# Macaron block (feed-forward, attention, feed-forward): transposes three and values four steps behind the scores, copies swapped between ScalarE and VectorE, side jobs spread anew

## The reference

```python
x = x + 0.5 * ffn(layernorm(x))          # x: 4 x 1024 tokens x 128
x = x + attn(layernorm(x))
x = x + 0.5 * ffn(layernorm(x))

def attn(x):                             # HEADS = 16, HEAD_DIM = 64, WINDOW = 64
    h = silu(x @ W1.T + b1) @ W2.T + b2
    q, k, v = split(h @ Wg.T + bg, 3)    # 3 * 16 * 64 columns
    dots = einsum('bhid,bhjd->bhij', q, k) * HEAD_DIM ** (-0.5)
    dots = where(j >= i + WINDOW, -inf, dots)
    out = einsum('bhij,bhjd->bhid', softmax(dots), v)
    return out @ Wo.T + bo

def ffn(x):                              # hidden 384
    return (silu(x @ wg.T) * (x @ wu.T)) @ wd.T
```

## Time and profile before

| | |
|---|---|
| median of 3 runs | 1632.81 us (1631.2 to 1634.49) |
| profiled execution | 1628.43 us, its span 1626.6 us, mean granted clock 0.976 |
| TensorE | 1439.0 us busy (88%), weight loads 1113.7 (68%) |
| GpSimd | 990.7 us (61%) |
| VectorE | 970.6 us (60%) |
| ScalarE | 776.3 us (48%) |
| DMA | 18 GB/s mean |

### The profile page before, as it was taken

The page is one execution under the profiler, slowest core; times in us unless marked ns, Lnnn a source line. Parts: engine busy times, 40 slices in busy tenths (PEclk is TensorE's granted clock), DMA queues, the critical chain, the costliest instruction groups (busy, mean ns, idle before and its releaser), DMA issues.

```text
span 1626.6 us, 38540 instructions
## 1 busy us (share of the span) xinstructions
PE 1439.0 (88%) x13330; PEld 1113.7 (68%) x13330; DVE 970.6 (60%) x1886; ACT 776.3 (48%) x1827; POOL 990.7 (61%) x592
## 2 busy tenths in 40 slices
PE   4767999999999999999999999999999999998676
PEld 3543777777777777777777777777777777777566
DVE  5653666666666666566666656666666656665444
ACT  2323555555555455554555555555555455454332
POOL 2231767677666667666676766677666666667410
PEclk9995999999999999999999999999999999999978
DMA  3100000000000000000000000000000000000000
GB/s 96 36 0 18 19 19 19 18 18 18 18 18 18 13 5 18 18 18 18 18 18 18 18 18 18 18 18 18 18 18 18 18 1 17 18 0 1 1 26 26
DMA packets 30571, 29.42 MB, mean 18 GB/s; under 512 B 6993, under 2 KB 25298, under 8 KB 30546
## 3 DMA queue, kind: packets, MB, share of 16 engines
q1 hardware_dynamic: 30546, 29.09, 5.9%
HBM read 8.07 MB, written 2.10 MB: 6 GB/s over the span
## 4 chain that ended last, share of the span: by engine, by line
PE 55%; issue 17%; DVE 13%; POOL 7%; ACT 6%; DVEq 1%; DMA 1%; ACTq 0%; POOLq 0%; SPq 0%
PE banks L773 16%; PE banks L754 15%; PE banks L789 8%; PE banks L719 6%; POOL probs L324 6%; ACT probs L389 5%; DVE probst L549 4%; DVE negmax L537 4%; PE banks L655 4%; PE banks L742 2%; PE banks L723 2%; DVE hidden L492 1%; PE banks L734 1%; POOL rstd_ln L295 1%; DVE xn_ln L478 1%
## 5 line engine op out<-in xcount | busy, mean ns | idle before, releaser
L324 POOL TENSOR_SCALAR probs<-probs,recips 128x704 f32<-128x704 f32 (+7 forms) x512 | 947.6, 1864 | 452.5 <-DVE recips L542 452.5
L537 DVE TENSOR_REDUCE negmax<-banks 128x1 f32<-128x704 f32 (+7 forms) x512 | 392.6, 808 | 129.8 <-PE banks L754 129.8
L773 PE MATMUL banks<-ident,probs 128*128 128x128 f32 x2752 | 391.4, 281 | 43.2 <-DVE probst L549 22.6
L397 ACT ACTIVATE probst<-banks 128x512 f32<-128x512 f32 (+1 forms) x320 | 177.4, 555 | 516.2 <-PE banks L773 516.2
L389 ACT ACTIVATE probs<-banks,negmax 128x704 f32<-128x704 f32 (+7 forms) x512 | 397.2, 785 | 44.5 <-DVE negmax L537 44.5
L773 PEld LDWEIGHTS banks<-ident,probs 128*128 128x128 f32 x2752 | 293.2, 141 | 130.3 <-issue 69.3
L549 DVE COPY probst<-banks 128x512 f32<-128x512 f32 (+1 forms) x416 | 276.6, 665 | 171.8 <-PE banks L773 169.8
L789 PE MATMUL banks<-probst,vs 128*64 128x128 f32 x5504 | 357.0, 277 | 0.8 <-ACT probst L397 0.8
L789 PEld LDWEIGHTS banks<-probst,vs 128*64 128x64 f32 x5504 | 295.3, 137 | 37.6 <-issue 22.5
L754 PE MATMUL banks<-kt,qt 64*128 64x512 f32 (+4 forms) x2496 | 298.3, 365 | 3.1 <-issue 3.1
L754 PEld LDWEIGHTS banks<-kt,qt 64*128 64x128 f32 x2496 | 206.0, 186 | 50.5 <-issue 5.8
(11 more groups left out here) (58 smaller groups left out, 881.1 us busy)
## 6 DMA issues: line engine op xcount, KB each, us to landing
hslot<-h_sb SPq DMA_DIRECT2D x32, 512.0 KB, 3.2
wslot<-in_wqkvt SPq DMA_DIRECT2D x32, 128.0 KB, 3.0
wslot<-wq_sb SPq DMA_DIRECT2D x32, 64.0 KB, 2.6
y<-xres SPq DMA_DIRECT2D x8, 256.0 KB, 2.3
wo_sb<-in_wot SPq DMA_DIRECT2D x1, 512.0 KB
wq_sb<-in_wqkvt SPq DMA_DIRECT2D x1, 512.0 KB
bslot<-bqk_sb SPq DMA_DIRECT2D x32, 1.0 KB, 1.9
iload<-in_wgatet SPq DMA_DIRECT2D x1, 192.0 KB, 2.4
```

The lines of the kernel that those rows point to most:

```text
L324: nc.gpsimd.tensor_scalar(here, here, recips[:, c, h:h + 1], None, ALU.mult).then_inc(normed.sem, 1)
L397: nc.scalar.activation(probst[c % 2][:, 4 * g:4 * g + w, :].rearrange("p t q -> p (t q)"), banks[:, TRANSPOSED[g % 2], 0:w * P], ACT.Copy) ...
L537: nc.vector.tensor_reduce(negmax[:, c, h:h + 1], src, AX.X, ALU.max, negate=True).then_inc(maxed.sem, 1)
L773: last = nc.tensor.transpose(banks[:, TRANSPOSED[g % 2], (t - 4 * g) * P:(t - 4 * g + 1) * P], probs[c, h][:, kb * P:(kb + 1) * P], ident[:])
```

## The change

`T_LAG` goes from 2 to 3 and `PV_LAG` from 3 to 4. ScalarE copies the even groups of transposes and VectorE the odd ones. On ScalarE the copy of group 0 stands ahead of the exponentials. On VectorE the reciprocal now stands ahead of the step's jobs, and the first job ahead of the copy of group 3. On TensorE the first job of a step comes after the value products, a second one after all transposes. The jobs get new steps; v0 and v1 are made in the turn that uses them, and no longer before the first turn; o1 joins o2 and o3 behind the drain.

```diff
-    T_LAG, PV_LAG = 2, 3
+    T_LAG, PV_LAG = 3, 4
-    JOBS = {0: ["k0"], 1: ["o2", "q0"], 2: ["k1"], 3: ["o3", "q1"], 4: ["v0"], 5: ["o0"], 6: ["v1"], 7: ["o1"]}
+    JOBS = {0: ["o1"], 1: ["v0"], 2: ["o2"], 3: ["v1"], 4: ["o3", "k0"], 5: ["q0"], 6: ["o0", "k1"], 7: ["q1"]}
...
-        taken = [T("taken_vector", [(c, g) for c in range(STEPS) for g in range(0, groups[c], 2)]),
-                 T("taken_scalar", [(c, g) for c in range(STEPS) for g in range(1, groups[c], 2)])]
+        taken = [T("taken_scalar", [(c, g) for c in range(STEPS) for g in range(0, groups[c], 2)]),
+                 T("taken_vector", [(c, g) for c in range(STEPS) for g in range(1, groups[c], 2)])]
...
-        def job_turn(job, c, i):
-
-            return i + 1 if job[0] in "kqv" else i - 1 if job in ("o2", "o3") else i
+        def job_turn(job, i):
+
+            return i + 1 if job[0] in "kq" else i - 1 if job in ("o1", "o2", "o3") else i
+
+        def runs(job, carry, more):
+            return more if job[0] in "kq" else carry or job[0] == "v" or job == "o0"
...
@@ ScalarE, step @@
-                if turning and groups[tc] > 1:
-                    take(tc, 1, ti)
-                if here:
-                    exps(c, i)
+                if turning:
+                    take(tc, 0, ti)
+                exps(c, i)
                 if carry or c >= PV_LAG:
                     attention_out(ac, ai)
-                if turning and groups[tc] > 3:
-                    take(tc, 3, ti)
+                if turning and groups[tc] > 2:
+                    take(tc, 2, ti)
...
@@ VectorE, step @@
                 row_max(c, i)
-                if turning:
-                    take(tc, 0, ti)
-                for job in JOBS[c]:
-                    if job[0] == "o" and (carry or job in ("o0", "o1")):
-                        add_output(job, job_turn(job, c, i))
-                if turning and groups[tc] > 2:
-                    take(tc, 2, ti)
+                if turning and groups[tc] > 1:
+                    take(tc, 1, ti)
                 invert(c, i)
-                for job in JOBS[c]:
-                    if job[0] == "v" and more:
-                        values(job, i + 1, 1 - r)
-                    if job[0] in "kq" and more:
-                        queries_keys_low(job, i + 1, 1 - r)
+                for job in JOBS[c][:1]:
+                    evict(job, i, r, carry, more)
+                if turning and groups[tc] > 3:
+                    take(tc, 3, ti)
+                for job in JOBS[c][1:]:
+                    evict(job, i, r, carry, more)
...
-            values("v0", 0, 0)
-            values("v1", 0, 0)
...
-            add_output("o2", TURNS - 1)
-            add_output("o3", TURNS - 1)
+            for name in ("o1", "o2", "o3"):
+                add_output(name, TURNS - 1)
...
@@ TensorE @@
-                if c == 0:
-                    pe.wait_ge(v_done.sem, v_done.after("v1", i))
+
+                pe.wait_ge(v_done.sem, v_done.after("v0" if blocks[c] <= 4 else "v1", i))
...
                 score(c, i, r)
                 if turning:
                     turns_of(tc, ti, (0, 1))
-                for job in JOBS[c]:
-                    if job[0] == "o":
-                        do(job)
                 if attending:
                     attend(ac, ai, r if c >= PV_LAG else 1 - r)
+                do(JOBS[c][0])
                 if turning:
                     turns_of(tc, ti, (2, 3))
-                for job in JOBS[c]:
-                    if job[0] != "o":
-                        do(job)
+                for job in JOBS[c][1:]:
+                    do(job)
...
-            for name in proj.events:
+            for name in ("k0", "q0", "k1", "q1"):
```

More of the change, by code:

```diff
@@ L435, in _ @@
             for c in range(PV_LAG):
-                tail_step = c
                 ti, tc = back(TURNS, c, T_LAG)
@@ L439, in _ @@
                 if c < T_LAG:
-                    take(tc, 1, ti)
+                    take(tc, 0, ti)
                 attention_out(ac, ai)
-                if c < T_LAG:
-                    take(tc, 3, ti)
+                if c < T_LAG and groups[tc] > 2:
+                    take(tc, 2, ti)
             copy_transposed(pd, "ln1", 0)
@@ L580, in step, with evict @@
                 row_max(c, i)
[L581 to L593 removed]
+                if turning and groups[tc] > 1:
+                    take(tc, 1, ti)
+                invert(c, i)
+                for job in JOBS[c][:1]:
[4 more added lines that the diff above has]
+                    evict(job, i, r, carry, more)
+            def evict(job, i, r, carry, more):
+                if not runs(job, carry, more):
+                    return
+                if job[0] == "o":
+                    add_output(job, job_turn(job, i))
+                elif job[0] == "v":
+                    values(job, i, r)
+                else:
+                    queries_keys_low(job, i + 1, 1 - r)
             for name in qk_done.events:
                 queries_keys_low(name, 0, 0)
[L597 to L598 removed]
             for c in range(STEPS):
@@ L802, in step @@
                 turning, attending = carry or c >= T_LAG, carry or c >= PV_LAG
-                def runs(job):
-                    return more if job[0] in "kqv" else carry or job in ("o0", "o1")
                 def do(job):
-                    if not runs(job):
+                    if not runs(job, carry, more):
                         return
                     k = JOB_ORDER.index((c, job))
-                    earlier = [(s, name, i) for s, name in JOB_ORDER[:k] if runs(name)]
-                    s, name, t = earlier[-1] if earlier else (*JOB_ORDER[-1], i - 1)
-                    misc_read(name, job_turn(name, s, t))
-                    n = job_turn(job, c, i)
-                    if job[0] in "kqv":
-                        project(job, n, 1 - r)
+                    earlier = [(name, i) for _, name in JOB_ORDER[:k] if runs(name, carry, more)]
+                    name, t = earlier[-1] if earlier else (JOB_ORDER[-1][1], i - 1)
+                    misc_read(name, job_turn(name, t))
+                    n = job_turn(job, i)
+                    if job[0] == "o":
+                        output(job, n)
                     else:
-                        output(job, n)
+                        project(job, n, r if job[0] == "v" else 1 - r)
                 score(c, i, r)
@@ L864, in _ @@
                     turns_of(tc, ti, (2, 3))
+            misc_read("o0", TURNS - 1)
+            output("o1", TURNS - 1)
             misc_read("o1", TURNS - 1)
```

24 lines of the change are left out of this document (12 added, 12 removed).

## The result

| | before | after |
|---|---|---|
| median | 1632.38 us, 4 runs | 1779.7 us, 4 runs (1774.93 to 1783.96) |
| ratio | | 1.09, 95% interval 1.0868 to 1.0932 |
| span of the profiled execution, granted clock | 1626.6 us, 0.976 | 1779.7 us, 0.938 |
| one turn in the middle (28 turns) | 43.02 us | 48.15 us |

The change costs 147.3 us. I had forecast 40, and a range that ended at 1702. The page after the change: the busy times, the granted clock in 40 slices, and the queue that brings instructions (packets, MB, share).

A forecast was written before the change was run, and what follows sets the result against it. TensorE's one stream of matmuls was taken as the bound. Turns of 44.4 us, 1.4 more, add 42 us over 30 turns; one-time terms -2. With 40 added to the 1632.8 median, the forecast was 1673 us, range 1650 to 1702.

The forecast's parts named there:

- the holes: TensorE's idle gaps in each middle turn: forecast to grow from 4.4 us to 5.63 us, making a turn 44.4 us.
- the terms that come once: Prologue without v0 and v1 saves 5.7 us, turn 0 costs 0.8 and the drain 2.8; together -2.
- the step 4 chain: Step 4: k0 waits for VectorE's addition behind the reciprocal, starting at t = 3.55; hole 1.80 us in place of 0.72.
- the masks in step 5: Step 5: masks done at 3.20 with 2.70 us of TensorE work; hole 0.50 us in place of 0.29 and 0.71.
- k1 in step 6: Step 6: k1 waits for the addition after o0, until t = 4.12; hole 1.37 us in place of 0.76.
- the turn's end: Step 7 into next step 0: scores wait for q1's low half until 5.81; holes 0.08 and 1.88 us.
- Holes not where I put them: Rival: additions reach TensorE before it asks in steps 4 and 6; 1556, or 1610 with only these hidden; chance 0.09.
- VectorE's low half blocked by GpSimd: Rival, step 7: q1's low half waits for GpSimd's 1024-column instruction, hole 1.8 us a turn larger; 1727; chance 0.03.
- The holes spread: Rival: close VectorE meetings of k and q jobs with maxima in steps 5 and 6 slip 0.5 us each; 1703; chance 0.10.
- The clock: Rival: new holes of 1.4 to 1.9 us drop TensorE to 1.2 GHz; time past 1750; chance 0.02.
- rule on weight loads pulled ahead: Loading weights early would save up to 0.19 us at each of three waits, 17 us, giving 1656; forecast rejected it.
- The deeper stagger: One more step between scores and transposes, so GpSimd's tile is ready: removes the 0.52 us hole in step 1.

The follow-up runs named there:

- experiment 3: Changed kernel, shifted by 119 unused instructions at the head of TensorE's list, with extra matmuls filling three holes a turn; 1707.48 us, ratio 1.0458.
- experiment 1: Changed kernel with 154 unused semaphore instructions at the head of TensorE's list, so its turn loop begins elsewhere (the shifted changed kernel); 1746.32 us, ratio 1.0716.
- 2: Kernel before the change, with 128 unused instructions at the head of TensorE's list so its loop begins half a block later; 1724.82 us, ratio 1.0564.
- 12: Kernel of 10 without its 72 extra instructions at the head of TensorE's list, nothing else changed; 1639.45 us, ratio 1.005.
- experiment 11: Changed kernel with lags put back to 2 and 3, shifted by 72 unused instructions at the head of TensorE's list; 1671.11 us, ratio 1.0244.
- experiment 8: As experiment 1, but the swap of copies undone: VectorE copies the even groups and ScalarE the odd again; 1776.21 us, ratio 1.0879.
- 4: As experiment 1, but VectorE does an o job's addition ahead of the reciprocal; 1683.56 us, ratio 1.0318.
- experiment 5: As experiment 1, but only the job table changed: k0 alone, q1 a step earlier, o0 last; 1677.16 us, ratio 1.0277.
- 10: Experiment 1 with experiment 5's table, additions before reciprocal (paired: before odd copy), paired o jobs before value products, lags 2 and 3, 72 extra instructions; 1539.65 us, ratio 0.9431.

## Why the prediction was wrong

The direction held and the chain it rested on is there, but the sum left two costs out, the code fetched again and the lower clock, and undersized the third, the holes. The 147.3 us divide like this. Earlier first masks (143.62 for 147.40) give 3.8 back. Longer turns at full clock cost 71.4, 30 times 45.40 less 43.02, by experiment 3. The low clock costs 33.5 (experiment 3 against 1), the code fetched again 43.2, with the low clock that it brings (experiment 1, its late start taken off). Together 144.3; 3.0 remain for turn 0 and the drain. The profiled executions put more there. Turn 0, from the first masks to the next turn's first scores, takes 40.60 us for 37.32, 3.3 more where I had 0.8. From the last turn's first scores to the end it is 156.4 for 151.4, 5.0 more where I had 2.8. With 3.8 for 5.7 at the first masks, the terms that come once are +4.5 in place of the forecast -2.

**Code fetching: a step that the prediction doesn't have.** "Adds none to a turn and takes none away" is true of matmuls, and I read no further. The prologue that became shorter had only its 5.7 us counted as gain. Experiments 1, 2 and 12 show the effect in three schedules, in both directions, with the packets as its mark: 15 or 16 where the loop begins at 3.79 or 3.92 blocks, 141 where it begins at 3.32, 3.64 or 4.29. Which beginnings are kept isn't explained. Counted as here, the kept loops touch 8 blocks, and of the fetched ones two touch 7. Only if the blocks began 55 to 88 instructions ahead of where I count from would all kept loops touch 7 and all fetched ones 8; no run shows that offset.

**"It stays at 1.00 through holes up to 0.71 us by the rows; three of 1.4 to 1.9 a turn are new."** That sentence was right and its chance, 0.02, was not. I had no row of such a hole at full speed and treated that as evidence against, so the sum has nothing for a term of 33.5 us. "The time would pass 1750" came with help from the other cause: without its 43 us the kernel would stand near 1736.

**The holes.** Forecast 44.4 us a turn, measured 45.40 with the clock held. In the changed kernel the step 4 chain reads, on VectorE:

```profile
737.34 0.41 DVE L551 COPY probst<-banks 128x256 f32<-128x256 f32 x1
738.62 0.17 DVE L544 RECIPROCAL recips<-sums 128x2 f32<-128x2 f32 x1 [0.86 <-ACT probs L394]
738.90 0.42 DVE L576 TENSOR_TENSOR xres<-banks,xres 128x256 f32 x1
```

The addition starts 0.28 behind the reciprocal, where I took 0.12 from the value copy, and TensorE starts k0 at 739.47, 0.15 behind its end, where I took 0.06. From the start of the transposes at 735.64 to k0 are 3.83 us, forecast 3.55. The stated bound for such a place, up to 0.2 more, covers the first; the second had no bound. On the mean of the turns at full clock in experiment 1 the places are 3.85 for 3.55 (k0 in step 4), 3.21 for 3.20 (the masks in step 5), 4.32 for 4.12 (k1 in step 6; 4.25 in the turn that begins at 712.86) and 5.88 for 5.81 at the turn's end, 0.6 us in all of the missing 1.0. Another 0.3 is work. I gave k and q jobs 0.1 more behind value products, but the other jobs pay it too: the o job at 737.03 stands there and lasts 0.71 us, the one at 762.05 behind transposes 0.61. In the changed kernel o1, o2 and one v job more stand behind value products in steps without a hole. The last 0.1 stays open.

The steps, from first score to first score, means in us at full clock:

| | 0 | 1 | 2 | 3 | 4 | 5 | 6 | 7 | turn |
|---|---|---|---|---|---|---|---|---|---|
| before | 5.21 | 6.41 | 4.46 | 4.94 | 4.86 | 5.20 | 6.02 | 5.91 | 43.02 |
| changed (experiment 1) | 4.40 | 5.41 | 5.36 | 4.84 | 6.21 | 4.76 | 6.94 | 7.47 | 45.4 |
| the same, lags 2 and 3 (experiment 11) | 4.84 | 5.63 | 4.05 | 4.15 | 6.21 | 4.77 | 6.99 | 7.68 | 44.32 |

The last chain has its rows on ScalarE and VectorE as forecast, high half and then low half:

```profile
711.34 0.68 ACT L385 ACTIVATE qt<-banks,bslot 128x512 fp32r<-128x512 f32 x1
```

```profile
712.05 0.75 DVE L559 SCALAR_TENSOR_TENSOR qt<-banks,bslot,qt 128x512 fp32r<-128x512 f32 x1 [1.18 <-ACT qt L385]
```

**The rivals.** *Holes not where I put them*: fell, by both waits. *VectorE's low half blocked by GpSimd*: fell. The low half above runs inside this instruction of GpSimd, 0.03 us behind its input and in 0.75 us:

```profile
711.08 5.67 POOL L329 TENSOR_SCALAR probs<-probs,recips 128x1024 f32<-128x1024 f32 x2 [1.93 <-DVE recips L544]
```

By its operands the low half reads one of its two tensors from PSUM (`banks`), so it isn't the case of two SBUF inputs that the prediction names, and that rule would not have given this rival's time. *The holes spread*: its size (1703) is near experiment 3, by other means. *The clock*: came. The Trainium skill's rule on weight loads pulled ahead (TensorE: Matmul & The Clock Gate, Architectural detail) saves nothing at these waits: the load of k0 waits too, and both it and the first matmul start at 739.47.

```profile
739.47 0.30 PEld L727 LDWEIGHTS banks<-hslot,wslot 128*128 128x128 f32 x2 [1.92 <-DMA bslot<-bqk_sb]
```

**The parts of the change.** Its parts have different signs. The swapped copies gain (experiment 8: 30 us). The new place of the addition loses 63 (4), and the change's table loses 69 against the one of experiment 5, each by itself against the shifted changed kernel and with the low clock that goes with it; against the table of before it wasn't measured. The deeper stagger, which I credited with 0.52 us a turn for GpSimd, loses 67 there and 23 in the better order (11 and 10, the earlier starts of 8 and 12 us taken off). By the count of tiles it moves four of transposes and four of products for each head out of steps 4 to 7, whose exponentials are the long ones, into steps that TensorE's work fills already. The table of steps shows it: with either lags steps 4 to 7 take 25.4 to 25.7 us, since their chains end them, while steps 0 to 3 take 20.0 us with the deeper stagger and 18.7 without. That account predicted the direction of experiment 11 and overstated the gain in the turn by 0.7 us. What took away the wait for GpSimd wasn't the lag, since it is absent with lags 2 and 3 as well; which other part did wasn't tried.

## What to carry to other kernels

An output that another job will overwrite has to be read out before anything on that engine which waits for the step's long chain, and its producer belongs ahead of work that nobody waits for. Both moves here cost no instruction. With the swapped copies, the table of experiment 5, the old lags and a loop whose code is kept they make a kernel 5.7% faster than before. A deeper stagger isn't free slack: count which steps the moved work leaves, and whether these were the ones that needed cover. And when a loop on TensorE is as long as this one, some 1700 instructions, look at the instruction queue's packets in each profile. If they grow with the passes, move the loop's beginning before drawing any conclusion on the schedule.

## What the runs showed of the hardware

- A loop of 1701 to 1711 TensorE instructions ran without fetching code again (15 packets) or fetched 9 packets a pass (141), with a stall of up to 3.9 us at each jump back, by its beginning alone. The Trainium skill (Advanced Engine Details and Errata, ISA Cache) gives 128KB for TensorE, in lines of 256 instructions, but also says "Only 2 cache lines!". By two lines every pass would be fetched again; these traces don't agree with that, since 6.6 to 6.9 blocks were kept in eleven of the kernels.
- The lower clock came in some kernels behind waits of 1.3 to 1.8 us, with TensorE busy otherwise: with three such waits a turn (21 stretches in experiment 1), with two of 1.5 us on average (8 in experiment 5) and with one of 1.8 (15 in experiment 4). It came with all 14 stalls of experiments 2 and 12. It did not come in experiment 11, whose three waits a turn were 1.0, 1.3 and 1.7 us, nor in those with waits of 0.7 at most. What tips it isn't settled.
- 46 and 50 us in stalls turned into 100 and 83 us (experiments 12 and 2, the late start taken off) in kernels that otherwise kept full speed, since each stall also took the clock.
- 154 idle semaphore instructions on TensorE delayed its first matmul by 9.9 us, and 72 by 0.2, since the first matmul waits for VectorE until 17 us anyway. From 119 to 154 of them it came 5.3 us later, 0.15 us for each.
